# GNN + attention + FFN layer on one core: in-degrees summed as rows by TensorE, and side jobs of two stages moved to other places

## What is computed

```
xn  = layernorm(x)
deg = segment_sum(ones, dst);  deg_inv = 1 / max(deg, 1)
mean(h) = segment_sum(h[src], dst) * deg_inv[:, None]
h   = relu(xn @ W_self0 + mean(xn) @ W_neigh0 + b0)
gnn = h @ W_self1 + mean(h) @ W_neigh1 + b1
x   = x + gnn + attention(xn)        # linear attention, relu on q and k
x   = x + ffn(layernorm(x))          # 1024 -> 4096 -> 1024, weights rounded to -1, 0, 1 times a scale
```

## Time and profile before

| | |
|---|---|
| time, median of 3 runs | 1288.99 us (1288.76 to 1289.01) |
| profiled execution, its own time | 1288.99 us |
| profiled execution, span from first to last instruction | 1287.2 us |
| PE busy | 1282.2 us, 6562 matmuls |
| DVE busy | 884.6 us |
| ACT busy | 664.2 us |
| POOL busy | 97.1 us |
| PE on the chain that ended last | 96% |

### The profile page before, as it was taken

The page is one execution under the profiler, slowest core; times in us unless marked ns, Lnnn a source line. Parts: engine busy times, 40 slices in busy tenths (PEclk is TensorE's granted clock), DMA queues, the critical chain, the costliest instruction groups (busy, mean ns, idle before and its releaser), DMA issues.

```text
span 1287.2 us, 19324 instructions
## 1 busy us (share of the span) xinstructions
PE 1282.2 (100%) x6562; PEld 631.5 (49%) x6562; DVE 884.6 (69%) x1565; ACT 664.2 (52%) x938; POOL 97.1 (8%) x91
## 2 busy tenths in 40 slices
PE   9999999999999999999999999999999999999999
PEld 5454445555545445555444554444444444444444
DVE  6954452455567768997992994427887978786774
ACT  7765574456412336543432664547853377465460
POOL 0000000000000001120000100224540100000000
PEclk9999999999999999999999999999999999999999
DMA  9498987667235465645876448599949829732533
GB/s 359 147 268 262 294 268 216 209 226 245 100 115 196 146 207 179 207 137 198 281 249 220 137 134 261 149 352 255 320 134 378 260 71 296 181 73 66 131 56 109
DMA packets 170489, 260.39 MB, mean 202 GB/s; under 512 B 76192, under 2 KB 111776, under 8 KB 166816
## 3 DMA queue, kind: packets, MB, share of 16 engines
q1 hardware_dynamic: 158400, 251.36, 59.8%
q0 software_dynamic: 1440, 5.24, 2.3%
q10 hardware_dynamic: 10560, 2.62, 1.5%
HBM read 184.87 MB, written 57.55 MB: 188 GB/s over the span
## 4 chain that ended last, share of the span: by engine, by line
PE 96%; DVE 2%; DMA 1%; issue 0%; ACT 0%; DVEq 0%; ACTq 0%; SPq 0%
PE ps L2463 31%; PE ps L2819 14%; PE ps L2936 9%; PE ps L2899 8%; PE ps L2596 8%; PE ps L2724 8%; PE ps L2789 7%; PE ps L2771 5%; PE ps L2665 3%; PE ps L2515 1%; DMA AT<-Zb 1%; PE ps L2606 1%; PE ps L2497 1%; DVE AM L2276 0%; DVE Zb L2253 0%
## 5 line engine op out<-in xcount | busy, mean ns | idle before, releaser
L2463 PE MATMUL ps<-S,XH 128*128 128x512 f16 x960 | 209.0, 379 | 0.0
L2463 PEld LDWEIGHTS ps<-S,XH 128*128 128x128 f16 x960 | 93.5, 98 | 111.0
L2463 PE MATMUL ps<-S,Zb 128*128 128x512 f16 x480 | 106.7, 379 | 0.0
L2724 PE MATMUL ps<-XH,S 128*128 128x512 f16 (+1 forms) x576 | 105.7, 339 | 0.0
L2596 PE MATMUL ps<-XH,S 128*128 128x512 f16 (+1 forms) x576 | 102.6, 339 | 0.0
L2463 PE MATMUL ps<-Zb,XH 128*128 128x512 f16 x432 | 94.8, 379 | 0.0
L1141 ACT ACTIVATE AT<-ps 128x320 f16<-128x320 f32 x40 | 17.4, 434 | 142.0 <-PE ps L2463 86.9
L1811 DVE TENSOR_SCALAR STREAM<-tables,keys 128x320 f16 x240 | 71.0, 296 | 24.4 <-PE ps L2665 13.5
L2771 PE MATMUL ps<-XH,AT 128*128 128x512 f16 x400 | 86.7, 379 | 0.0
L2789 PE MATMUL ps<-AT,Zb 128*128 128x512 f16 (+1 forms) x480 | 84.7, 339 | 0.0
L2596 PEld LDWEIGHTS ps<-XH,S 128*128 128x128 f16 x576 | 56.1, 98 | 45.7
(11 more groups left out here) (346 smaller groups left out, 2157.1 us busy)
## 6 DMA issues: line engine op xcount, KB each, us to landing
STREAM<-in_w_all SPq DMA_DIRECT2D x48, 512.0 KB, 5.3
STREAM<-in_w1t SPq DMA_DIRECT2D x42, 512.0 KB, 5.1
STREAM<-in_w2t SPq DMA_DIRECT2D x28, 512.0 KB, 5.7
XIN<-in_x SPq DMA_DIRECT2D x20, 512.0 KB, 5.2
Zb<-in_w1t SPq DMA_DIRECT2D x14, 512.0 KB, 7.9
blocks_scratch<-S SPq DMA_DIRECT2D x4, 1792.0 KB, 8.5
blocks_scratch<-STREAM SPq DMA_DIRECT2D x4, 1792.0 KB, 8.5
S<-blocks_scratch SPq DMA_DIRECT2D x7, 1024.0 KB, 10.5
```

Source lines behind the costliest of these rows:

```text
L2463: last = mm(acc[:, n * BANK:(n + 1) * BANK], left(l, kc), right(kc, r)[:, n * BANK:(n + 1) * BANK], start=(kc == 0 and i == 0), stop=(kc = ...
L2724: last = mm(acc[:, n, :], W[:, kc, r, (c + 4 * n) * P:(c + 4 * n + 1) * P], XH[:, l, kc, unit_cols(u)], start=(kc == 0 and i == 0), stop=( ...
```

## The change

The degrees are no longer brought to partitions and sent round through DRAM to become a row. `deg_pe` now uses a 128 x 128 tile of ones (`iota_s`, which POOL overwrites with ones when all counts are made) as weights and the sums as 512, 512 and 256 columns, for the high and the low part: 6 matmuls whose result stands as a row on every partition, in banks 2, 3 and 7. `degrees` takes the maximum and the reciprocal over these 1280 columns and writes `inv_deg` itself; it is called in tile 9 of stage Z0 instead of tile 8. The 128 x 10 form, needed later for `deg_x`, is made from the row through DRAM during stage H. Besides, `SUMS_AT`, `N0_AT`, `S0_QUADS` and `H_QUADS` get other places, and in stage H the quad comes before `h_lows` and `h_sums` instead of after them.

```diff
-SUMS_AT = {2: (0,), 5: (1,), 8: (2,), 11: (3,)}
-N0_AT = (0, 1, 3, 4, 6, 7, 9, 10)
+SUMS_AT = {0: (0, 1), 8: (2,), 9: (3,)}
+N0_AT = (0, 1, 2, 3, 4, 6, 7, 8)
...
-        S0_QUADS = {0: 0, 2: 1, 3: 2, 5: 3, 6: 4, 8: 5, 9: 6}
-        H_QUADS = {0: EARLY_QUADS, 3: EARLY_QUADS + 1, 6: EARLY_QUADS + 2}
+        S0_QUADS = {0: 0, 1: 1, 3: 2, 4: 3, 5: 4, 6: 5, 9: 6}
+        H_QUADS = {1: EARLY_QUADS, 4: EARLY_QUADS + 1, 7: EARLY_QUADS + 2}
...
-            sp.wait_ge(S("deg_col"), 1)
-            sp.dma_start(deg_d.rearrange("(t p) -> p t", p=P), col("deg"), allow_slow_non_contiguous=True)\
-                .then_inc(S("deg_in"), 16)
-            sp.wait_ge(S("deg_in"), 16)
-            sp.dma_start(inv_deg, deg_d.partition_broadcast(P)).then_inc(S("deg_in"), 16)
...
+                if u == 1:
+                    sp.dma_start(deg_d, inv_deg[0:1, :]).then_inc(S("deg_in"), 16)
+                if u == 3:
+                    sp.wait_ge(S("deg_in"), 16)
+                    sp.dma_start(col("deg"), deg_d[0].rearrange("(t p) -> p t", p=P), allow_slow_non_contiguous=True).then_inc(S("deg_in"), 16)
...
-            for i in range(EDGE_QUADS):
+            for i in range(EARLY_QUADS):
+                last_blocks(i)
+            pool.wait_ge(S("at"), NG)
+            nc.gpsimd.memset(iota_s, 1.0).then_inc(S("iotas"), 1)
+            for i in range(EARLY_QUADS, EDGE_QUADS):
                 last_blocks(i)
...
-                link(V.tensor_scalar(col("deg"), ps[:, DEG_AT:DEG_AT + 2 * NT].rearrange("p (t e) -> p t e", e=2)[:, :, 0],
-                                     1.0, None, ALU.max))
-                V.reciprocal(col("deg"), col("deg")).then_inc(S("deg_col"), 1)
                 for j in range(2):
                     dve.wait_ge(S(f"rows_out{j}"), 8 * NT + 8 * UNITS)
+                link(V.tensor_scalar(inv_deg[:, 0:D], banks(2), 1.0, None, ALU.max))
+                link(V.tensor_scalar(inv_deg[:, D:NP_], banks(7, cut=NP_ - D), 1.0, None, ALU.max))
+                link(V.reciprocal(inv_deg, inv_deg))
...
-                if t == NT - 2:
+                if t == NT - 1:
...
-                if u == 0:
-                    dve.wait_ge(S("deg_in"), 32)
...
+                if u - 1 in H_QUADS:
+                    quad(H_QUADS[u - 1])
                 if u > 0 and u != UNITS - 2:
                     h_lows(u - 1)
                 h_sums(u)
-                if u - 1 in H_QUADS:
-                    quad(H_QUADS[u - 1])
...
+            dve.wait_ge(S("deg_in"), 32)
             times(col("deg_x"), col("deg"), col("tmp"))
...
-                for t in range(NT):
+                pe.wait_ge(S("iotas"), 4)
+                for to, at_, width in ((2 * BANK, 2 * P, BANK), (3 * BANK, 6 * P, BANK), (7 * BANK, 0, 2 * P)):
                     for n, part in enumerate((deg_hi, deg_lo)):
-                        last = mm(ps[:, DEG_AT + 2 * t:DEG_AT + 2 * t + 2], deg_part(part, t), one16[:, :],
-                                  start=(t == 0 and n == 0), stop=(n == 1), skip_group_check=True)
+                        last = mm(ps[:, to:to + width], iota_s, part[:, at_:at_ + width], start=(n == 0), stop=(n == 1))
```

More of the change, by code:

```diff
@@ L73 @@
 RING_QUADS = 19
-SUMS_AT = {2: (0,), 5: (1,), 8: (2,), 11: (3,)}
-N0_AT = (0, 1, 3, 4, 6, 7, 9, 10)
-DEG_AT = 7 * BANK
+SUMS_AT = {0: (0, 1), 8: (2,), 9: (3,)}
+N0_AT = (0, 1, 2, 3, 4, 6, 7, 8)
 M_BANK = {0: 6, 1: 6, 2: 6, 3: 6, 4: 6, 5: 2, 6: 4, 7: 6}
@@ L282, in gps_kernel @@
         s0_d = nc.dram_tensor("s0_scratch", (UNITS * P, D), F32, kind="Internal").ap()
-        deg_d = nc.dram_tensor("deg_scratch", (NP_,), F32, kind="Internal").ap()
+        deg_d = nc.dram_tensor("deg_scratch", (1, NP_), F32, kind="Internal").ap()
         st_d = [nc.dram_tensor(f"blocks{w}_scratch", (P, 7 * 4 * D), F16, kind="Internal").ap() for w in range(2)]
```

## The result

The changed kernel takes 1318.61 us (median of 4 runs, 1318.12 to 1320.92), the kernel before in the same comparison 1288.88. The ratio is 1.0234, 95% interval 1.0217 to 1.0252: slower by 29.7 us. The forecast was 1313.1, in a range of 1302 to 1322. The profiled execution took 1318.16, its span is 1316.1.

A forecast was written before the change was run, and what follows sets the result against it. PE, busy for the whole window, was taken to bound the kernel, so only its own work and waits count. 0.6 + 3.5 + 9.2 + 10.8 = 24.1 us on 1288.99 gave 1313.1, range 1302 to 1322.

The forecast's parts named there:

- Part 34: Late in stage S0: PE waits 0.4 us for this part of the one-hot rows.
- six matmuls and wait for `c_x` (Z0): Stage Z0: six matmuls replace 20 small ones, 0.6 us more; PE then waits 3.5 us for `c_x` before stage H.
- stage S0: Moved side jobs make DVE late with one-hot rows; PE's waits sum to 9.2 us, bounds 5 and 11.5.
- parts 21, 27, 30, 34: Parts of one-hot rows in stage S0 that PE waits for: 4.4, 1.1, 3.3 and 0.4 us.
- last unit of H: PE waits 5.9 us before unit 11, because DVE stands three times 4.4 us for ACT's rounding before a quad.
- first and third ST products: Behind stage H: `h_lows(9)` ends 2.8 us later, then `st_copy(0, 0)` costs PE 2.1 us more after two products.
- H and ST together: Waits from stage H's quad edits, in its last unit and behind: 10.8 us, bounds 9 and 12.6.
- The reciprocal: DVE, stage Z0, 1280 columns: 7.8 us at 6.0 ns a column; bounds 1.7 and 8.8 us.
- the eight passes of the Trainium skill: Alternative for the reciprocal: eight passes of 1.2 ns, an estimate of 12.3 us, a wait of 8.0, total 1317.6.
- rival 3: PE's clock falls in stalls of 4.4, 5.9 and 3.5 us, each adding up to 2.1: 1315.2 to 1319.4; chance 0.20.
- 1: DVE's idle time takes up all delays, only 0.6 us is left: 1289.6; decides at part 21; chance 0.06.
- 2: Only one of stages S0 and H runs late: 1302.3, or 1303.9 if stage S0 holds; chance 0.15.

The follow-up runs named there:

- a_fill: Against the changed kernel: matmuls of zeros on PE in front of part 21, the wait for `c_x` and stage H's last unit; 1313.78 us.
- a_no_recip: Against the changed kernel: the 1280-column reciprocal replaced by a multiplication with a constant; 1312.63 us.
- b_s0_new: Against the kernel before: only stage S0's three edits put in (`SUMS_AT`, `N0_AT`, `S0_QUADS`); 1300.48 us.
- a_deg_only: Against the changed kernel: side jobs of stages S0 and H back at their old places, only the change of the degrees left; 1297.86 us.
- The three kernels that do one part each: The degrees alone, stage S0's three edits alone, and stage H's two edits alone, the rest as in the kernel before; 1297.86, 1300.48 and 1300.38 us.
- a_deg_tile8: Against the changed kernel: side jobs at their old places, and `degrees` called in tile 8 of stage Z0 instead of tile 9; 1291.20 us.
- b_h_early: Against the kernel before: both stage H edits put in, with ACT rounding each quad a unit earlier; 1291.36 us.
- b_sums_n0: Against the kernel before: new `SUMS_AT` and `N0_AT` put in, `S0_QUADS` as it was; 1289.49 us.
- b_n0_quads: Against the kernel before: new `N0_AT` and `S0_QUADS` put in, `SUMS_AT` as it was; 1302.39 us.
- b_squads: Against the kernel before: new `S0_QUADS` alone put in, quads 1 and 3 to 5 a tile earlier; 1297.57 us.

## Why the prediction was right, and where not

**The places and the releasers** were right: the six matmuls, `c_x`, parts 21, 27 and 30, the last unit of stage H, `h_lows(9)` and `st_copy`. Part 34, put at 0.4, came too: PE is 0.3 us late at it, and with the slower matmuls behind it 0.45 us are lost.

**The terms** against the changed kernel and against a_fill, where PE's clock is 1.00 (us; "filled" where the zero matmuls stand in the gap; a gap between matmuls less 0.2 for the matmul itself):

| term | forecast | after | a_fill |
|---|---|---|---|
| six matmuls and wait for `c_x` (Z0) | 4.1 | 4.5 | 4.5 |
| stage S0 | 9.2 | 11.65 | 8.3 |
| of it parts 21, 27, 30, 34 | 4.4, 1.1, 3.3, 0.4 | 4.5, 1.3, 2.3, 0.3 | filled, 1.3, 1.4, 0.2 |
| last unit of H | 5.9 | 5.9 | filled |
| first and third ST products | 2.8, 2.1 | 0.7, 2.0 | 2.6, 2.0 |
| H and ST together | 10.8 | 12.0 | 10.5 |

**The reciprocal.** The forecast took 7.8 us, by 6.0 ns a column, and it took 8.15, while the two maxima before it took 1.65 and not 1.9. PE's wait for `c_x` is 3.7 us, 3.5 were forecast. The profile after, by groups:

```profile
L1967 DVE RECIPROCAL HL<-HL 128x1280 f32<-128x1280 f32 x1 | 8.2, 8153 | 0.0
```

The extrapolation from 10 columns to 1280 by the earlier trace rows held within 5%, though nothing in the rows said that it would. The estimate from the eight passes of the Trainium skill (VectorE: DVE Perf Modes, "First, the fixed hardware budget"), 12.3 us and a total of 1317.6, comes near the total for a wrong reason: the operation did not take 12.3 us.

**Stage S0.** At part 21 the forecast's own steps can be checked one by one in the timelines of ACT and DVE:

```profile
494.61 2.17 ACT L1181 ACTIVATE Zb<-Zb,cols 128x1024 f32<-128x1024 f32 x2
496.69 1.14 ACT L971 ACTIVATE S<-SPLIT,cols 128x1024 f16<-128x1024 f32 x1
```

```profile
497.86 1.28 DVE L1537 SCALAR_TENSOR_TENSOR S<-SPLIT,cols,S 128x1024 f16<-128x1024 f32 x1 [2.00 <-ACT S L971]
499.06 1.22 DVE L1917 TENSOR_SCALAR Zb<-Zb 128x2048 fp8e4<-128x2048 f32 x1
500.31 1.23 DVE L1920 TENSOR_TENSOR Zb<-Zb 128x1024 fp8e4<-128x1024 fp8e4 x1
501.82 0.99 DVE L1814 TENSOR_SCALAR STREAM<-tables,keys 128x320 f16 x1 [0.28 <-issue]
...
504.86 0.92 DVE L1885 TENSOR_SCALAR HL<-ps,cols 128x226 f32<-128x226 f32 x2
```

ACT's high half ended at 497.83 (forecast 497.9) and DVE had the part done at 504.9 (504.8). At part 30 the chain runs, as forecast, over SP's late load of quad 4:

```profile
532.26 8.26 DMA Zb<-in_w1t
540.55 1.24 ACT Zb L1177
```

The term of 3.3 us was too large: 2.3 in the changed kernel, and 1.4 in a_fill, a_no_recip and b_s0_new, where the same transfer took 7.30 to 7.36 us and not 8.26.

**Stage H.** DVE's wait in front of each quad, forecast 4.4 us three times, in the kernel after:

```profile
DVE STREAM L1917 <- ACT STREAM L1181: 12.9, 3, 4.3
```

The hold of the low parts by POOL is there too (1.92 for the L2041 pair at 738.53), and the sum, 10.8, is met by 10.5 in a_fill.

**The step that failed** is the weight between rival 3 and the forecast. The text gave 0.20 to the case that the clock falls in the stalls, because no stall of the trace before was long enough to show it, and the sum put it at nothing; it fell in each of the three long ones, and that is most of the 5.5 us over the point. The rival's time, 1315.2 to 1319.4, holds the result. Its size of up to 2.1 us for a stall was low at part 21 (2.8, and 2.9 in front of stage H in a_deg_only) and high behind `c_x` in the changed kernel (1.5), and the third cost nothing, being inside the next wait. a_fill shows the fall as a cause: 4.8 of the 5.5 us by the medians, some 4 by the stages.

**Where luck helped.** That a_fill lies only 0.7 us from the forecast is in part luck. Its four stages together are 23.2 us longer than before, with 24.1 forecast: the term of part 30 was 1.9 too large there, the stall at part 21 and the wait for `c_x` a little too small. The other 2 us lie ahead of stage S0 and behind stage ST, of which the forecast says nothing.

**The rivals.** 1 falls, since the stalls came. 2 falls: each stage is late alone. The three kernels that do one part each account for the whole.

**No version beat the kernel before.** With PE busy throughout, a_deg_tile8, b_h_early and b_sums_n0 come to 2.1, 2.2 and 0.3 us over it.

## What to carry to other kernels

When one engine is the bound and never waits, a moved side job is priced by the first place at which another engine runs late for it, and that place is found by carrying the orders of the engines on, job by job, from the rows; here the quads had been put in front of what feeds TensorE while their own input was not ready. A long elementwise operation such as a reciprocal over a whole row belongs into an idle piece of its engine that is already there: one tile earlier it cost TensorE no wait. Behind stalls of TensorE of 3.7 us and more slow matmuls followed in this kernel, which cost 1.5 to 2.9 us: add them, unless the next wait takes them in.

## What the runs showed of the hardware

- The clock granted to PE was 0.50 behind stalls of 4.4, 3.7 and 5.7 us (and of 6.8 in b_n0_quads), with the next matmuls taking twice as long, and back near 1.00 some 3 to 6 us later; behind stalls of up to 2.8 us it stayed at 1.00 in the profiled executions. Executions of one kernel differed in how much of it they paid (a_deg_only, 1296.35 to 1298.98), and the mean clock of b_squads, whose longest stall is 2.8 us, was 1.000 in one execution and 0.997 in another. Matmuls of zeros in the stalls kept the clock at 1.00 (a_fill).
- A reciprocal of 128 x 1280 float32 took 8.15 us, 6.4 ns a column, a multiplication over the same tile 0.83 us.
- Two edits on one engine's order did not add up: 4.8 and 3.0 us alone, 11.3 together. DVE then waited 12.9 us for ACT and not 5.7, which made PE wait 5.7 us in front of the stage's last unit, where it didn't wait with either edit alone.
